# A ViT layer's loop: the jump announced at the body's head, and a pair's z transposes, logits and counts moved behind later projections

## The reference

```python
h = L0_tok_ref(x, W_proj, b_proj)                       # 16x16 patches to 192 numbers
h = concatenate([cls_tok, h], axis=1)                   # 197 tokens for each image
h = h + L0_attn_ref(layernorm(h), wq, wk, wv, wo, w_gate, w_up)
h = h + L0_ffn_ref(layernorm(h), gate_w, gate_b, gate_center, w1, b1, w2, b2)

# attention, for each of E = 4 experts: 12 heads of 16, window of 64 tokens
attn = softmax(where(mask, (q @ k.T) * scale, -1e30)); o = attn @ v
# feed-forward
p = softmax(x @ gate_w + gate_b - gate_center); expert = argmax(p)
out = w2[expert] applied to gelu(w1[expert] applied to x + b1[expert]) + b2[expert]
```

## Time and profile before

| | us |
|---|---|
| median of 3 executions | 5021.6 |
| lowest, highest | 5020.94, 5031.36 |
| the profiled execution: its own time | 5015.97 |
| the profiled execution: its span, first to last instruction | 5014.2 |
| PE, DVE, ACT, POOL busy in the span | 4221.2, 3866.1, 3232.3, 1197.4 |

### The profile page before, as it was taken

The page is one execution under the profiler, slowest core; times in us unless marked ns, Lnnn a source line. Parts: engine busy times, 40 slices in busy tenths (PEclk is TensorE's granted clock), DMA queues, the critical chain, the costliest instruction groups (busy, mean ns, idle before and its releaser), DMA issues. The chain is left out here.

```text
span 5014.2 us, 130984 instructions
## 1 busy us (share of the span) xinstructions
PE 4221.2 (84%) x47982; PEld 3226.5 (64%) x47982; DVE 3866.1 (77%) x8936; ACT 3232.3 (64%) x9686; POOL 1197.4 (24%) x1752
## 2 busy tenths in 40 slices
PE   4888888888888888888888888888888888886998
PEld 2666666666666666666666666666666666664776
DVE  5878887777777887778787888777777888875665
ACT  3677766666676776666667777666666777663433
POOL 1222222222222222222222222222222222221222
PEclk7999999999999998999999999999999999997999
DMA  5112121111111122111111222111111112212665
GB/s 181 27 45 50 50 50 49 46 45 44 39 32 48 50 50 49 45 46 45 46 28 43 50 50 50 50 47 44 45 44 25 47 50 50 50 48 104 219 215 170
DMA packets 246124, 309.21 MB, mean 62 GB/s; under 512 B 56426, under 2 KB 223892, under 8 KB 235651
## 3 DMA queue, kind: packets, MB, share of 16 engines
q1 hardware_dynamic: 221794, 227.65, 17.5%
q10 hardware_dynamic: 4608, 38.73, 2.3%
q0 software_dynamic: 18912, 32.58, 1.9%
HBM read 127.06 MB, written 43.10 MB: 34 GB/s over the span
## 5 line engine op out<-in xcount | busy, mean ns | idle before, releaser
L813 ACT ACTIVATE p_s<-bank,smin 128x128 f32<-128x128 f32 (+1 forms) x6144 | 1881.9, 397 | 229.1 <-DVE smin L902 183.6
L902 DVE TENSOR_REDUCE smin<-bank 128x3 f32<-128x384 f32 (+1 forms) x2048 | 1156.0, 566 | 275.1 <-PE bank L685 219.2
L699 PE MATMUL bank<-ident_s,p_s 69*69 69x69 f32 (+1 forms) x9216 | 1124.8, 250 | 199.4 <-DVE pt_f L908 173.4
L908 DVE TENSOR_TENSOR pt_f<-bank,pt_f 128x384 f16<-128x384 f32 (+1 forms) x2048 | 1142.8, 561 | 77.8 <-ACT pt_f L804 74.6
L804 ACT CAST pt_f<-bank 128x384 f16<-128x384 f32 (+1 forms) x2048 | 1072.6, 524 | 102.6 <-PE bank L699 102.3
L699 PEld LDWEIGHTS bank<-ident_s,p_s 69*69 69x69 f32 (+1 forms) x9216 | 821.8, 144 | 395.4 <-issue 196.0
L237 PE MATMUL bank<-v_f,pt_f 69*69 69x33 f16 (+1 forms) x18432 | 905.6, 185 | 0.0
L237 PEld LDWEIGHTS bank<-v_f,pt_f 69*69 69x69 f16 (+1 forms) x18432 | 849.4, 112 | 34.0 <-issue 8.3
L680 PE MATMUL bank<-masks_s,mask_id_s 128*128 128x384 f16 (+1 forms) x2048 | 698.7, 341 | 16.7 <-issue 10.7
L685 PE MATMUL bank<-stacks_f 128*128 128x256 f16 (+3 forms) x4096 | 702.9, 253 | 0.0
L842 POOL TENSOR_TENSOR o_e<-o_raw 128x192 f32<-128x192 f32 (+1 forms) x512 | 307.5, 601 | 1414.0 <-DVE o_raw L895 1414.0
(11 more groups left out here) (117 smaller groups left out, 4745.3 us busy)
## 6 DMA issues: line engine op xcount, KB each, us to landing
stacks_f<-qt_f SPq DMA_DIRECT2D x768, 73.9 KB, 2.1
stacks_f<-kt_f SPq DMA_DIRECT2D x1536, 36.9 KB, 2.1
wx_t<-wx_d SPq DMA_DIRECT2D x36, 1344.0 KB
x_raw<-x_t_dram ACTq DMA_DIRECT2D x32, 1182.0 KB, 8.1
rec_t<-rec_d SPq DMA_DIRECT2D x36, 678.0 KB
v_f<-v_f SPq DMA_DIRECT2D x64, 213.5 KB
rec_d<-fill_s SPq DMA_DIRECT2D x5, 678.0 KB, 4.1
stacks_f<-w_dram SPq DMA_DIRECT2D x2, 1536.0 KB
```

Of the source, the lines that this page charges most:

```text
L699: mm = nc.tensor.transpose(bank[T_BANK + u % TR][0:nk, b * nk:b * nk + rows], p_slot(u)[:, b * nk:b * nk + nk], ident_s[0:rows, 0:rows])
L813: ins = nc.scalar.activation(p_slot(s)[:, j * kn:j * kn + kn], bank[s % SR][0:rows, j * kn:j * kn + kn], ACT.Exp, scale=-1.0, bias=smin[0: ...
L902: nc.vector.tensor_reduce(least, ps, AX_X, ALU.min).then_inc(S["min_ready"], 1)
L908: nc.vector.tensor_tensor(pt[0:nk, u % PR, 1, 0:n], bank[T_BANK + u % TR][0:nk, 0:n], pt[0:nk, u % PR, 0, 0:n], ALU.subtract).then_inc(S[" ...
```

## The change

The loop is opened with `hint_back_edge=True`: at the top of every body each of the five engines issues one instruction more, a prefetch hint that names its loop-closing branch. And the six numbers grow: the z2 transposes and their way out by two products, logits and choice by two, counts and places by five.

```diff
-        AT_Z2, AT_Z2_OUT, AT_LOGITS, AT_CHOOSE, AT_COUNT, AT_PLACE = 4, 4, 8, 8, 13, 13
+        AT_Z2, AT_Z2_OUT, AT_LOGITS, AT_CHOOSE, AT_COUNT, AT_PLACE = 6, 6, 10, 10, 18, 18
...
-        with nc.Fori(0, STEPS) as i:
+        with nc.Fori(0, STEPS, hint_back_edge=True) as i:
```

## The result

The changed kernel takes 4871.7 us in the median of 4 runs (4863.3 to 4878.7), beside 5023.0 for the kernel before: a ratio of 0.9695 (95% interval 0.9676 to 0.9714), 3.0% faster. Forecast were 4820 us and 4.0%; the time lies outside the forecast's own range (4785 to 4860) and inside the wider one (4770 to 4910). The profiled execution spans 4871.1 us, 143 less than before.

A forecast was written before the change was run, and what follows sets the result against it. PE was taken as busiest, with long waits at the jump, for `onehot` and for z2. From 5016 us, 108 (jump) and 92 (projection stage) leave 4816, forecast as 4820; own range 4785 to 4860, wider 4770 to 4910.

The forecast's parts named there:

- The jump: Between two bodies: the hint removes the instruction fetch from PE's taken branch, 3.60 us to 0.08, saving 108 us.
- The hint's own price: At each body's head: one more sequencer instruction per engine, from nothing to 0.08 us, taken as 0.04.
- Rival 1: At the loop's back edge: the hint has no effect on PE, coming about 135 us early; 4928 us, chance 0.11.
- rival 4: Hint's early fetch pushes out the next block, engines fetch in mid-body, the branch still fetches: about 5205 us, chance 0.02.
- The start of the stage: Projection stage: products 4 and 5 fill PE's 1.89 us wait for z2; transposes still end at +8.75.
- The logits' wait: Projection stage: PE newly waits 2.4 us, +12.0 to +14.4, as ACT casts the pixels before z2.
- The walk: Projection stage followed engine by engine using the trace's durations; it put the first minimum at +25.8 before clock effects.
- Line 345: In the choice on DVE: the subtraction meets the end of POOL's line 860, taking 0.2 us instead of 3.21.
- The end of the stage: Last products to first minimum: `place` costs 1.14 us on DVE's path; first minimum at +25.8 before clock effects.
- its own signs of being wrong: Branch staying at 3.6 us, line 345 blocked with counts waiting, or first minimum to branch growing from 107 us.
- Rival 2: Projection stage gives only 60 us, half clock in every body, and ACT and DVE keep their fetches: 4874 us, chance 0.12.
- The clock: Behind the wait for logits: half clock in 4 bodies in 10, +0.5 us; 0.2 us allowed back at the jump.

The follow-up runs named there:

- e3: The changed kernel with counts and places behind product 15 instead of 18: 4800.7 us, ratio 0.957 to the kernel before.

## Why the prediction was right, and where it was not

- **The jump.** Right in mechanism, 98 us instead of 108. The hint's own price (0.04 taken, 0.03 measured) was fine; the mis-sized piece is what is left of the branch: a taken branch with a hint takes 0.36 us, not the 0.08 of one not taken. Rival 1 (no effect) and rival 4 (fetches that cost elsewhere) are refuted by the hint alone: branch 0.36 us, pipeline 106.98 us against 107.29.
- **The start of the stage.** Right: the transposes come at +7.0 as before, with six products ahead of them.
- **The logits' wait.** Expected 2.4 us, measured 1.80. The walk put DVE's first low part of z2 behind both of ACT's casts; it starts behind the first.
- **Line 345.** Right: 0.39 us instead of 3.21 (0.2 was taken), at +16.7, 0.35 us before POOL's line 860 ends.
- **The end of the stage.** First minimum forecast at +26.1, measured +25.77 in the mean, from +24.9 to +26.75. That it comes within 0.3 us is in part luck. The walk without half clock gave +25.8, and the 12 bodies that have none behind the logits' wait come at +25.02: the logits' wait was 0.6 us too long in it. Half clock was given to 4 bodies in 10, and it came in 20 of 32 (+26.22). The two misses point opposite ways.
- **What failed: "Scatter, POOL's, starts a little earlier than now and stays under the pipeline's first units."** It doesn't start earlier: from the first matmul it starts at +26.0 in the mean, where it was +24.7, and against the first minimum 4.6 us later. And the pipeline's units don't cover it: with it there, DVE starts minima late that nothing else holds back. Moving `place` by five products moved 5.3 us of issuing on POOL from the last low parts, with 0.27 us to spare before each in the body shown, to minima that the pipeline waits for. The prediction priced this overlap at nothing; the pipeline grew by 58 us, 71 more in its first eight units and 13 less behind them. That was one of its own signs of being wrong (a pipeline over 107 us; it is 109.10). The forecast took 200 us off and the traces 144: 58 here, 10 at the jump, less 12 that the stage gave beyond the forecast. Rival 2's time, 4874 us, is met to 2 us by chance: it had the stage giving 60 us (104 measured) and ACT and DVE keeping their fetches, which they lost. The trace of before showed the stall in small; DVE there, then POOL (the row between is in the earlier trace rows):

```profile
398.30 0.57 DVE L873 SCALAR_TENSOR_TENSOR qt_f<-bank,qt_f 128x394 f16<-128x394 f32 x1 [0.27 <-issue]
...
400.89 1.02 DVE L902 TENSOR_REDUCE smin<-bank 128x3 f32<-128x384 f32 x2 [0.87 <-PE bank L685]
```

```profile
399.00 1.17 POOL L387 DMA_INDIRECT rec_d<-rec,pos_u  x1 [0.30 <-issue]
```

  DVE is idle 0.87 us before the third minimum; the last indirect DMA ends at 400.17, within that gap. I had read PE's name in the bracket and passed on.
- **The clock.** Half clock at the logits' wait was allowed for; what wasn't is half clock in the first units. The two kernels without a scatter there have none, so it comes with the stall; but a stall doesn't always bring it (none in e3, with 9.41 us).

What stays open is why DVE stands. Shown is that the stall follows the scatter when it is moved, and goes when it goes; that in 26 of 32 bodies of the changed kernel its last long wait ends 0.4 to 0.9 us behind the end of the fourth indirect DMA on POOL, so it outlasts the issuing; and that there the first two of the four don't hold back the minima at 381.15 to 384.15 above. It isn't every DVE instruction either: before the change the low part at 398.30 started at its usual pace beside the third. The scatter's moving data can't be all of it, since in 23 of 32 bodies the first minimum that starts over 0.9 us late was due before the scatter's first packet moved. The Trainium skill (SBUF — State Buffer, the shared port pair) names GpSimd and VectorE as rivals for one pair of ports, for a VectorE instruction in a two-port mode or with two SBUF inputs. That fits line 345; line 902 has a single input, in PSUM, and stands all the same. So either the cause is another than these ports, or the measurement goes further than the page. Whether ports, descriptors or something else is held wasn't tried.

## What to carry to other kernels

A block that is moved takes its successors on other engines with it: list what each engine issues behind its last semaphore, indirect DMAs on POOL above all, and ask what DVE does in that stretch. An idle bracket whose releaser ended a microsecond earlier may name the wrong cause; look at which engine was busy through the gap. And where a loop's back edge shows a fetch, as PE's branch of 3.60 us does here, try hinting the jump: here one argument took 3.2 us off every turn.

## What the runs showed of the hardware that I had not expected

- Four indirect DMAs in a row on POOL can make DVE start instructions late, though these read PSUM: unit 5's minimum starts 1.8 to 3.2 us behind its last matmul with them there, 0.08 us without. The first eight units take 7.91 us without, 9.5 to 10.95 with them at full clock, and up to 12.3 with half clock.
- A taken branch on PE takes 0.36 us hinted and 3.6 us unhinted, and the hint holds from the body's head to its end, 135 us and some 2,900 matmuls and weight loads later.
- Moving counts and places by one product, from 15 to 16 with z2 first, changed the number of bodies with half clock in the first units from 1 to 20 of 32.
